# Graph attention on one core: the low parts of v and the row constants move from GpSimd to VectorE, read straight from PSUM

## The reference

```python
q = x @ Wq.T + bq
k = x @ Wk.T + bk
v = x @ Wv.T + bv
scores = q @ k.T / sqrt(128)
scores = where(adj > 0, scores, -9e15)
att = softmax(scores, axis=-1) @ v
out = layernorm(x + elu(att))
```

## Time and profile before

| what | value |
|---|---|
| time, median of 3 runs | 434.38 us (434.34 to 434.85) |
| profiled execution, time | 434.82 us |
| profiled execution, span of the trace | 433.0 us |
| PE busy | 419.7 us (97%), 3470 matmuls |
| VectorE busy | 361.0 us (83%) |
| ScalarE busy | 354.0 us (82%) |
| GpSimd busy | 354.2 us (82%) |
| mean granted TensorE clock | 0.997 |

### The profile page before, as it was taken

One profiled execution on the slowest core, in us unless ns is written; L12 is line 12 of the kernel. 1 busy time (PEld: TensorE's weight loads), 2 busy tenths in 40 slices (PEclk: granted clock), 3 DMA queues, 4 the chain that ended last, 5 costly groups with the idle time before them and its releaser, 6 DMA issues.

```text
span 433.0 us, 11489 instructions
## 1 busy us (share of the span) xinstructions
PE 419.7 (97%) x3470; PEld 309.0 (71%) x3470; DVE 361.0 (83%) x677; ACT 354.0 (82%) x742; POOL 354.2 (82%) x644
## 2 busy tenths in 40 slices
PE   7897999999999999999999999999999999999994
PEld 6653677777777777777777777777777777777784
DVE  2778899888888988888889888888888888888784
ACT  4886769888888898888888888888888988888893
POOL 0497459888988898889888988898889888898875
PEclk9999999999999999999999999999999999999998
DMA  8954999999999999999999999999999999998551
GB/s 225 383 194 82 257 260 250 238 260 272 264 253 281 259 258 245 276 271 260 245 265 272 263 242 266 275 260 251 257 275 256 249 259 284 260 255 231 102 85 39
DMA packets 149649, 104.77 MB, mean 242 GB/s; under 512 B 132738, under 2 KB 141444, under 8 KB 141444
## 3 DMA queue, kind: packets, MB, share of 16 engines
q1 hardware_dynamic: 149200, 104.41, 91.4%
q10 hardware_dynamic: 436, 0.20, 0.2%
HBM read 69.47 MB, written 2.10 MB: 165 GB/s over the span
## 4 chain that ended last, share of the span: by engine, by line
POOL 62%; issue 15%; PE 13%; ACT 4%; DVE 4%; POOLq 2%; ACTq 0%; DVEq 0%
POOL p_rows L403 29%; POOL res L417 6%; POOL neg_mean L428 4%; POOL rstd L441 4%; POOL var_eps L439 3%; POOL y L422 3%; POOL att_sum L410 3%; PE ps_out L960 3%; POOL att L412 3%; POOL centred L430 2%; POOL expm L419 2%; POOL y_out L445 2%; PE ps_scores L921 2%; PE ps_scores L922 1%; PE ps_scores L923 1%
## 5 line engine op out<-in xcount | busy, mean ns | idle before, releaser
L403 POOL TENSOR_TENSOR p_rows<-scores,p_rows 128x256 f16<-128x256 f32 x252 | 176.2, 730 | 7.2 <-ACT p_rows L560 7.2
L687 DVE CUSTOM_DVE_ANT_0 scores<-ps_scores,adj 128x1024 f32<-128x1024 f32 x128 | 156.0, 1219 | 19.6 <-issue 13.6
L543 ACT ACTIVATE scores<-scores,neg_max 128x1024 f32<-128x1024 f32 x128 | 145.7, 1138 | 3.4 <-DVE neg_max L697 3.4
L703 DVE TENSOR_TENSOR p_lo<-ps_t,p_hi 128x512 f16<-128x512 f32 x124 | 82.6, 685 | 26.4 <-ACT p_hi L552 24.5
L673 DVE TENSOR_SCALAR adj<-adj 128x1024 f32<-128x1024 int32 x128 | 99.6, 779 | 0.2 <-DMA adj<-in_adj_dram 0.2
L921 PE MATMUL ps_scores<-k_hi,q_hi 128*128 128x512 f16 x256 | 97.0, 379 | 1.9 <-DVE q_lo L654 1.6
L923 PE MATMUL ps_scores<-k_hi,q_lo 128*128 128x512 f16 x256 | 97.0, 379 | 0.0
L922 PE MATMUL ps_scores<-k_lo,q_hi 128*128 128x512 f16 x256 | 97.0, 379 | 0.0
L960 PE MATMUL ps_out<-v_parts,p_hi 128*128 128x256 f16 x496 | 95.4, 273 | 0.8 <-DVE p_lo L703 0.8
L960 PE MATMUL ps_out<-v_parts,p_turned 128*128 128x256 f16 x496 | 95.0, 273 | 0.0
L552 ACT ACTIVATE p_hi<-ps_t 128x512 f16<-128x512 f32 x122 | 71.7, 587 | 21.8 <-PE ps_t L937 18.9
(11 more groups left out here) (121 smaller groups left out, 481.9 us busy)
## 6 DMA issues: line engine op xcount, KB each, us to landing
adj<-in_adj_dram SPq DMA_DIRECT2D x64, 1024.0 KB, 5.4
out_dram<-y_out SPq DMA_DIRECT2D x32, 64.0 KB, 5.0
x_rows<-in_x_dram SPq DMA_DIRECT2D x4, 256.0 KB, 4.3
x_rows<-in_x_dram SPq DMA_DIRECT2D x2, 512.0 KB, 7.1
p_turned<-p_rows SPq DMA_TRANSPOSE x63, 4.5
w_rows<-in_L_gnn_Wq_dram ACTq DMA_DIRECT2D x1, 64.0 KB, 2.7
w_rows<-in_L_gnn_Wk_dram ACTq DMA_DIRECT2D x1, 64.0 KB, 3.3
w_rows<-in_L_gnn_Wv_dram ACTq DMA_DIRECT2D x1, 64.0 KB, 4.7
```

The source lines that it names most:

```text
L403: last = nc.gpsimd.tensor_tensor(p_rows[c][:, w:][:, cols], s_sb[s][:, c * PIECE:c * PIECE + w][:, cols], p_rows[c][:, 0:w][:, cols], ALU. ...
L543: nc.scalar.activation(s_sb[s][:, cols], s_sb[s][:, cols], ACT.Exp, bias=neg_max[:, s:s + 1], accum_out=p_sums[:, s, c:c + 1]).then_inc(ex ...
L687: nc.vector.tensor_tensor_reduce(out=s_sb[s][:, cols], in0=ps_scores[c % 2][:, :], in1=mask_sb[s][:, cols], scale=SCALE, scalar=-3.0e38, o ...
L703: nc.vector.tensor_tensor(p_lo[:, k, :], ps_t[bank_of(s, g)][:, :], p_hi[:, k, :], ALU.subtract).then_inc(plo_ready, 1)
```

## The change

The float32 copy of v in SBUF is gone, and with it ScalarE's first copy of each group and `v_sb`. ScalarE makes only the high part. VectorE gets a new function `low_of_v(g)`: it waits for that high part, subtracts it from the same PSUM bank for up to three tiles at once, and adds row_b to the 129th column in PSUM. GpSimd loses all 11 groups; what is left for it in the opening are the low parts of blocks 6 and 7 of k and `row_logs(0)`. PE now waits for `v_lo`, which VectorE raises behind its second instruction, before it writes a bank again. In VectorE's order the calls stand behind `masked_piece` (and `row_max`) of their step and ahead of the step's `mask_piece`s: groups 0 to 3 in step 3, 4 and 5 in step 4, 6 in step 5, 7 and 8 in step 6, 9 in step 7, 10 in step 0 of period 1. PE's order is unchanged.

```diff
@@ gpsimd
-            pool.wait_ge(row_copied, 2)
-            for g in range(V_GROUPS):
-                tiles = v_tiles(g)
-                n = len(tiles)
-                pool.wait_ge(v_copied, 2 * g + 2)
-                for part in (slice(0, 2), slice(2, n))[0:n - 1]:
-                    to = slice(tiles[0] + part.start, tiles[0] + part.stop)
-                    last = nc.gpsimd.tensor_tensor(v_parts[:, to, 0:D], v_full(g)[:, part, 0:D], v_parts[:, to, D:2 * D],
-                                                   ALU.subtract)
-                nc.gpsimd.tensor_tensor(row_free[:, tiles[0]:tiles[0] + n],
-                                        v_full(g)[:, :, D:D + 1].rearrange("p b a -> p (b a)"),
-                                        row_b[:, 0:1].to_broadcast([P, n]), ALU.add).then_inc(row_added, 1)
-                last.then_inc(v_lo, 1)
-                if g < STEPS - X_FIRST:
-                    low_of_k(X_FIRST + g)
-                if g == 2:
-                    row_logs(0)
+            for g in range(X_FIRST, STEPS):
+                low_of_k(g)
+            row_logs(0)
@@ scalar, copy_v
-                nc.scalar.activation(v_full(g), ps_v(g), ACT.Copy).then_inc(v_copied, 1)
                 nc.scalar.activation(v_parts[:, tiles[0]:tiles[0] + len(tiles), D:2 * D], ps_v(g)[:, :, 0:D],
                                      ACT.Copy).then_inc(v_copied, 1)
@@ vector
             def hold_rows(n):
                 tiles = slice(*ROW_GROUPS[n])
-                dve.wait_ge(row_added, 1 if n == 0 else V_GROUPS)
+                dve.wait_ge(v_lo, 1 if n == 0 else V_GROUPS)
...
+            def low_of_v(g):
+                tiles = slice(v_tiles(g)[0], v_tiles(g)[-1] + 1)
+                dve.wait_ge(v_copied, g + 1)
+                if g == 0:
+                    dve.wait_ge(row_copied, 2)
+                nc.vector.tensor_tensor(v_parts[:, tiles, 0:D], ps_v(g)[:, :, 0:D], v_parts[:, tiles, D:2 * D], ALU.subtract)
+                nc.vector.tensor_scalar(row_free[:, tiles], ps_v(g)[:, :, D:D + 1].rearrange("p b a -> p (b a)"),
+                                        row_b[:, 0:1], None, ALU.add).then_inc(v_lo, 1)
@@ vector, period
                     if has_scores and not warm and p == 0:
+                        if j == 3:
+                            for g in range(V_FIRST):
+                                low_of_v(g)
+                        for g in v_at(j):
+                            low_of_v(g)
...
                     elif has_scores:
+                        if not warm:
+                            for g in v_at(STEPS * p + j):
+                                low_of_v(g)
@@ tensor, project_q
-                    pe.wait_ge(v_copied, 2 * V_GROUPS)
+                    pe.wait_ge(v_lo, V_GROUPS)
@@ tensor, project_v
-                    pe.wait_ge(v_copied, 2 * g - 2)
+                    pe.wait_ge(v_lo, g - 1)
```

More of the change, by code:

```diff
@@ L89, in attention_kernel @@
         v_parts = sb("v_parts", [P, TILES, VW], F16)
-        v_sb = sb("v_sb", [P, V_GROUPS - 8, V_TILES, D + 1], F32)
         adj_sb = [sb(f"adj{n}", [P, N], I32) for n in range(2)]
@@ L140, in attention_kernel @@
         row_copied = sem("row_copied")
-        row_added = sem("row_added")
         row_held = sem("row_held")
@@ L238, in v_at @@
             return [g for g in V_AT if V_AT[g] == t]
[L240 to L247, removed]
         ROW_GROUPS = ((0, V_TILES), (V_TILES, TILES))
```

## The result

The changed kernel takes 439.9 us (median of 4 runs, 439.5 to 440.5) against 434.36: 1.0129 times as long, with an interval of 1.0115 to 1.0142, or **5.5 us slower**. The forecast was 438.2 with a range of 436.9 to 440.4. The profiled execution takes 439.88 us with a span of 437.7, so of its 5.1 us over the one of before 4.7 lie in the span and 0.4 around it (2.18 against 1.82 us).

A forecast was written before the change was run, and what follows sets the result against it. PE was taken to bound the loop from 60 us on, so the opening's delay moves the end: 4.07 us later minus 0.25 from GpSimd's interference gives 3.8, so 434.38 + 3.8 = 438.2 us, range 436.9 to 440.4.

The forecast's parts named there:

- The bound and the place: PE alone bounds the loop from 60 us on; any delay of the opening (periods 0 and 1) moves the end equally.
- The new wait: Opening: PE's group 2 of v waits for low_of_v(0), starting at 21.05 instead of 16.79, 4.26 us later.
- 0.5 less: Favourable end for the long mask at 17.63 (1.21 us) beside GpSimd's low_of_k: 0.5 us off the loss.
- VectorE's instructions: Added per v group: subtraction 0.55 us, next after 0.47; row constant 0.16, next after 0.09; 11 groups are 6 us.
- The clock: PE's clock falls in the 4.1 us hole ahead of group 2, costing about 2 us more: 440.2; chance 0.17.
- The shift of the chain: Opening: tile 0's last masked piece 4.3 us later, low part of q's block 1 at 34.05, 4.07 later.
- What VectorE's freedom from GpSimd gives back: Masks between q's block 1 and period 2 run shorter beside idle GpSimd: 0.25 us back, ends 0 and 0.6.
- rival 1: PE's clock falls in the hole ahead of group 2 of v, about 2 us more: 440.2; chance 0.17.
- rivals 2 and 3: 2: period 1's holes absorb the delay, 436.8 to no change, chance 0.06; 3: quieter GpSimd frees VectorE and PE, 432.1, 0.03.
- The amount is not what hurts; the place is.: VectorE has room for 6 us between 14 and 43 us; the call's place behind step 3's masked piece costs time.

The follow-up runs named there:

- e4_hole_only: Kernel before, with one added wait holding PE's group 2 of v until the second masked piece is done; 439.20 us (+4.5).
- e3_sbuf_copy: Kernel before, with GpSimd's v subtraction moved to VectorE, reading the SBUF copy; ScalarE's copies and PE's waits as before; 438.81 us (+4.1).
- a8_low0_first: Changed kernel, v groups 3 to 10 one per step, low part of group 0 ahead of first masked piece, group 1 behind it; 436.01 us (+1.7).
- a6_spread_early: Changed kernel, low parts of groups 0 and 1 behind first masked piece, v groups 3 to 10 spread one per step; 436.62 us (+2.1).
- e1_filler: Changed kernel with 26 throwaway transposes on PE ahead of group 2 of v, to fill the hole; 439.39 us (+4.7).
- e2_early_low: Changed kernel with low parts of groups 0 and 1 behind the first masked piece instead of the second; 437.82 us (+3.1).
- e7_pool_pad: Changed kernel with 32 tiny memsets on GpSimd behind row_logs(0), restoring its number of instructions; 439.33 us.
- e5_after: The changed kernel measured once more, with nothing further changed; 440.31 us (+5.8).

## Why the prediction was right, and where its sum was short

- **The bound and the place.** Right for 4.4 of the 5.1 us of the profiled execution. PE is full from 60 us on before and after, and what the opening loses stays. The other 0.7 us lie behind the last store and around the span, which the prediction took as fixed.
- **The new wait.** Right in its mechanism: PE's group 2 waits for `low_of_v(0)` behind the masked piece of step 3. Predicted start 21.05, measured 20.51. Of the 0.54 us between, 0.26 come from the earlier adj (first mask at 15.31 instead of 15.57) and 0.17 from the mask behind it (1.04 instead of 1.21 us); PE started 0.05 us behind the end of the row constant, where the prediction took some 0.15 for a reaction and no row of its own showed it. The end "0.5 less" of the prediction named the mask alone; that the adj landed earlier as well was luck.
- **VectorE's instructions.** The subtraction takes 0.55 us and the next follows after 0.47, as taken. The row constant takes 0.21 instead of 0.16, and the next instruction follows after 0.12 instead of 0.09.
- **The clock.** This is the term that was left out of the likeliest sum. It had a chance of 0.17 and a price of 2 us; it happened in every profile of the changed kernel (mean clock 0.992 in each), and its price is about 1.2 us. The reasons given against it were no rows but doubts: that there was one instance of a fall, 3.3 us after PE went quiet, that it may come later after other work, and that a shorter hole would be different. The hole was longer than 3.3 us by the prediction's own walk. The Trainium skill (TensorE: Matmul & The Clock Gate, Part 1) says that an idle array drops to 1.2 GHz and needs sustained work to come back. The trace agrees with both: the clock is at 1.2 GHz from 21.0 us, behind the hole of 3.49 us, and comes back at about 24.5 with PE busy throughout from 20.51. The fall itself came half a microsecond after PE had started again.
- **The shift of the chain.** From the second masked piece to the low part of q's block 1 the prediction walked 14.99 us (19.06 to 34.05). With filler the traces have 14.94 and 14.86. So without the clock the walk was right within 0.15 us.
- **What VectorE's freedom from GpSimd gives back.** Between 34 and 50 us the distance to before shrinks from 4.76 to 4.44 us, so by 0.32, where 0.25 was taken: the masks' median is 0.685 instead of 0.742 us.
- **The sum by the runs.** For the profiled execution 4.07 was forecast at the low part of q's block 1. Measured is 4.76: 0.43 less for the second masked piece, which started at 18.63 and not at 19.06, and about 1.2 more for the clock. Then 0.32 come back, and PE's last matmul is 4.38 late. With 0.35 behind the last store and 0.36 around the span that makes 5.1 us, against 3.8 forecast. The range to 440.4 holds 439.9 because it took in half of rival 1; the time at the end of the program stood in no term, and the early masked piece made up for part of it.
- **The rivals 2 and 3.** Neither showed. PE's hole in period 1 is still there (0.92 us ahead of 38.23, again ended by a low part of q), and no gain from a quieter GpSimd appears beyond the 0.3.
- **"The amount is not what hurts; the place is."** Right for the changed kernel as it stands: e4_hole_only, with the wait and without the work, loses 4.25 us at PE's last matmul against 4.38. But the work has a price as soon as the wait is gone. It puts tile 0's last masked piece 2.6 us later in e3_sbuf_copy, and it is the likely cause of the 0.7 to 0.8 us that a8_low0_first still loses in the opening. The room that VectorE had (5 us between 18 and 44) was not all where the work could stand.

## What to carry to other kernels

When work moves to another engine, don't ask only whether that engine has room, but what stands ahead of the moved step in its order and which engine's next buffer now hangs on it; here one call behind one masked piece stopped TensorE for 3.5 us. Price a hole in TensorE ahead of dense work with a fall of the clock on top (about 1.2 us here), and test for it by filling the hole with throwaway matmuls. An engine that is 82% busy and on nobody's path is a good place for such work even if another could do it in fewer instructions. And compare the end of the program too, behind PE's last matmul and around the span: 0.7 us of 5.1 were there, where nothing of the change runs.

## What the runs showed of the hardware that was not expected

The clock doesn't fall in the hole but can fall when TensorE is already back at work: in a6_spread_early the hole is 2.15 us long and ends at 18.88, and the windows of 2 us around it are:

```profile
18.00:20.00 2.00, 1.12 (x7) 0.87 (x8) 2.00 (x7) 0.26 (x2) 1.50 (x3) 0.92 0.99 418
20.00:22.00 2.00, 2.00 (x9) 1.59 (x8) 1.78 (x5) 0.35 (x1) 0.00 (x0) 0.50 0.66 274
```

0.92 means that the lower level held for the last 0.3 us of the first window, so the fall came at about 19.7, 0.8 us into new work, and behind a hole of only 2.15 us. So the 3.3 us of the earlier trace rows can't be taken as a length below which a hole is safe. The hole of 1.41 us in e1_filler had no fall behind it; what lies between, no run here settles.

The changed kernel can also be held up by the landing of the first adj tile, which differs from run to run. In the profile of e2_early_low VectorE waited 2.10 us for it, and the mask, the masked piece, the low part of group 0 and then PE's group 2 (at 19.64) followed one upon the other. By moving the release of v's buffers behind VectorE's first masked pieces the change ties TensorE to that DMA. In the four profiles of the changed kernel itself it matters little: the first mask starts at 14.96 (e7_pool_pad) to 15.64 us (e5_after), but the second masked piece at 18.61 to 18.63 in three of them and PE's group 2 at 20.50 or 20.51. In e7_pool_pad both are 0.3 us earlier, and so is PE's group 1, which doesn't wait for adj.
